# Shared down product in three rounded terms, and a new order of the second expert's weight loads

## The reference

```python
scores = softmax(x_flat @ gate_w.T); w = scores * in_top2
h = silu(g) * u                    # per expert, I = 352
out = sum over experts of (h @ experts_down[e].T) * w[:, e]
shared = (silu(x_flat @ shared_gate_w.T) * (x_flat @ shared_up_w.T)) @ shared_down_w.T   # SI = 704
out = out + sigmoid(x_flat @ shared_expert_gate_w.T) * shared
```

## Time and profile before

| | |
|---|---|
| median of 3 runs | 480.49 us (479.61 to 480.49) |
| the profiled execution | 479.78 us, of which the span in the trace is 478.1 us |
| PE busy | 462.0 us, 97% of the span |
| DVE, ACT, POOL busy | 287.1, 201.8, 242.8 us |
| chain that ended last | PE 83%, DVE 6%, ACT 4%, issue 2%, DMA 2% |

### The profile page before, as it was taken

One profiled execution on the slowest core, in us unless ns is written; L12 is line 12 of the kernel. 1 busy time (PEld: TensorE's weight loads), 2 busy tenths in 40 slices (PEclk: granted clock), 3 DMA queues, 4 the chain that ended last, 5 costly groups with the idle time before them and its releaser, 6 DMA issues.

```text
span 478.1 us, 9570 instructions
## 1 busy us (share of the span) xinstructions
PE 462.0 (97%) x3166; PEld 382.7 (80%) x3166; DVE 287.1 (60%) x651; ACT 201.8 (42%) x452; POOL 242.8 (51%) x324
## 2 busy tenths in 40 slices
PE   7999999999999999999999999999998899999996
PEld 6777767687777788779999999999987667767685
DVE  5879986562353122335455545545556779999895
ACT  3555775477620022003332332233232555676752
POOL 6323443155337557267895553233231665766654
PEclk9999999999999999999999999999999999999999
DMA  8999600020002223999913333222116400000104
GB/s 275 388 411 353 96 13 1 1 88 2 0 1 93 85 70 107 309 281 218 314 38 110 101 100 89 70 68 76 47 39 203 158 1 2 2 2 0 45 14 165
DMA packets 48144, 53.00 MB, mean 111 GB/s; under 512 B 15425, under 2 KB 42370, under 8 KB 47842
## 3 DMA queue, kind: packets, MB, share of 16 engines
q1 hardware_dynamic: 38562, 29.51, 22.0%
q0 software_dynamic: 7664, 20.19, 12.7%
q10 hardware_dynamic: 1872, 2.69, 1.8%
HBM read 35.25 MB, written 17.12 MB: 110 GB/s over the span
## 4 chain that ended last, share of the span: by engine, by line
PE 83%; DVE 6%; ACT 4%; issue 2%; DMA 2%; POOL 0%; SPq 0%; ACTq 0%; POOLq 0%; DVEq 0%
PE banks L1263 12%; PE banks L1316 10%; PE banks L347 6%; PE banks L1367 6%; PE banks L325 5%; PE banks L1368 5%; PE banks L1371 5%; PE banks L361 5%; PE banks L314 4%; PE banks L336 3%; PE banks L1389 3%; PE banks L1390 3%; PE banks L1393 3%; PE banks L1379 3%; PE banks L978 2%
## 5 line engine op out<-in xcount | busy, mean ns | idle before, releaser
L1201 ACT ACTIVATE hg<-banks 128x352 f32<-128x352 f32 x39 | 18.1, 465 | 98.4 <-PE banks L1371 98.4
L115 POOL TENSOR_TENSOR rstd<-var,mhalf 128x2 f32<-128x2 f32 x30 | 20.8, 695 | 74.7 <-DVE var L108 74.7
L1541 DVE TENSOR_TENSOR hgT_lo<-banks,hgT_hi 128x256 fp32r<-128x256 f32 x78 | 24.1, 350 | 56.3 <-ACT hgT_hi L1208 56.3
L1367 PE MATMUL banks<-w_hi,xgT_hi 128*128 x156 | 54.7, 351 | 0.1
L515 DVE TENSOR_REDUCE mx<-banks 128x16 f32<-128x1024 f32 x32 | 39.1, 1221 | 20.9 <-PE banks L325 20.7
L1368 PE MATMUL banks<-wd,xgT_hi 128*128 x156 | 50.3, 323 | 0.0
L1316 PE MATMUL banks<-sdn,big 128*128 128x256 f32 x192 | 47.5, 393 | 0.0
L1316 PEld LDWEIGHTS banks<-sdn,big 128*128 128x128 f32 x192 | 34.1, 189 | 12.6 <-issue 9.0
L1098 POOL DMA_INDIRECT expert_rows_in<-xn,slot x32 | 31.4, 980 | 18.4 <-issue 6.7
L325 PE MATMUL banks<-kvb,qT 64*128 64x256 f32 x256 | 36.3, 401 | 2.2 <-DVE pw L518 0.9
L1371 PE MATMUL banks<-w_hi,xgT_lo 128*128 x156 | 37.6, 322 | 0.0
(11 more groups left out here) (250 smaller groups left out, 1163.8 us busy)
## 6 DMA issues: line engine op xcount, KB each, us to landing
w_hi<-in_egu POOLq DMA_DIRECT2D x2, 2816.0 KB, 21.6
expert_rows_in<-zeros SPq DMA_DIRECT2D x1, 5304.0 KB, 40.9
xn<-expert_rows_in SPq DMA_DIRECT2D x39, 128.0 KB, 2.1
y_all<-choices_out SPq DMA_DIRECT2D x16, 256.0 KB, 5.2
wd<-in_egu SPq DMA_DIRECT2D x4, 704.0 KB, 7.2
out_x<-x SPq DMA_DIRECT2D x7, 256.0 KB, 2.3
x<-in_x SPq DMA_DIRECT2D x2, 768.0 KB, 7.4
wd<-in_edown POOLq DMA_DIRECT2D x4, 384.0 KB, 6.6
```

Source lines behind the costliest of these rows:

```text
L1367: nc.tensor.matmul(to, xgT_hi[:, c, k, :], hi, start=(k == 0), stop=False)
```

## The change

It does four things. (1) The shared down product is done in three terms, as the others are: ACT rounds the hidden rows (`high_part`) and the weights `sdn` (`round_shared_down`), POOL (slices 0 to 7) or DVE (the rest) makes the hidden rows' low part (`low_part`), DVE that of the weights (`split_shared_down`), and `down(g)` has 72 products of float32r. `hidden` is now on DVE for all slices, and ACT's copy of the up half is gone. (2) `down(0)` stands ahead of `up(8)`, where it stood behind `up(11)`, and `rank_choices` stands behind `up(8)`. (3) Expert 1's weights are loaded by SP and POOL after `down(2)` is done (`d_ready` 12) instead of by ACT and POOL after `up(23)`; their low parts are both made by POOL, `make_w_lo(1)` no longer by DVE. (4) The weights of the second attention are loaded behind all experts' weights, since their memory holds `sdn_hi` now, and the list `products` is weighted anew.

```diff
+        weights_at = nc.sbuf_base - 3 * KD * D * 4
+        hT_hi, hT_lo, hT_more, sdn_hi, sdn_lo = [
+            nc.alloc_sbuf_tensor_at(name, shape, F32R, offset=at) for name, shape, at in (
+                ("hT_hi", [P, KS, SG], big_at), ("hT_lo", [P, KS, SG], big_at + KS * SG * 4), ("hT_more", [P, 2, 2, SG], turned_at),
+                ("sdn_hi", [P, KS, D], weights_at), ("sdn_lo", [P, KS, D], sdn_at))]
...
+        act_s = mem["pw"]
+        FACTORS, BY_POOL = 4, 8
+        HELD_IN = [0, 1, 2, 3, 4, 5, 6, 7, 0, 1, 2, 3, 4, 5, 8, 9, 6, 7, 0, 1, 2, 3, 10, 11]
+        def h_part(n, lo):
+            at = HELD_IN[n]
+            if at < KS:
+                return (hT_lo if lo else hT_hi)[:, at, :]
+            if at < KS + 4:
+                return (xn2T_lo if lo else xn2T_hi)[(at - KS) // 2][:, (at - KS) % 2, :]
+            return hT_more[:, at - KS - 4, lo, :]
+        def wait_low_part(engine, n):
+            if n < BY_POOL:
+                wait(engine, h_done, n + 1)
+            else:
+                wait(engine, h2_done, n - BY_POOL + 1)
...
-            wait(sp, events["q_ready"], Q_STEPS)
-            wait(sp, events["wo_ready"], NU)
-            for dst, src in ((wk, wk1), (wv, wv1), (wq[1], wq1), (wo[1], wo1)):
-                sp.dma_start(dst[:, :, :], split(src)).then_inc(attn1_in, 16)
             sp.wait_ge(scattered, 16 * 2 * NT)
             for b in range(NX):
                 fetch(sp, b)
+            sp.wait_ge(d_ready, 12)
             sp.wait_ge(d_in, 16 * KI)
-            sp.wait_ge(w_in[1], 16 * KD)
+            load_w(sp, 1, 2, w_in[1])
+            load_d(sp, 1, 2, 1, d_in)
+            sp.wait_ge(d_in, 32 * KI)
             load_w(sp, 2, 4, w_in[2])
             load_d(sp, 2, 4, 1, d_in)
             for b in range(NX, NX + 3):
                 fetch(sp, b)
-            sp.wait_ge(h2_done, 2 * KS)
-            sp.wait_ge(ranked, 1)
+            sp.wait_ge(d_ready, 16)
...
+            for dst, src in ((wk, wk1), (wv, wv1), (wq[1], wq1), (wo[1], wo1)):
+                sp.dma_start(dst[:, :, :], split(src)).then_inc(attn1_in, 16)
             for b in range(NX + 5, NB):
                 fetch(sp, b)
...
+            def low_part(n):
                 rows = slice(0, SR[n % KS])
-                wait(pool, silu_done, n + 1)
-                wait(pool, u_copied, n + 1)
-                nc.gpsimd.tensor_tensor(hT[rows, (n // KS + 1) % 2, n % KS, :], up_s[rows, n % 2, :],
-                                        act_s[rows, n % 2, :], ALU.mult).then_inc(h_done, 1)
+                wait(pool, hi_done, n + 1)
+                nc.gpsimd.tensor_tensor(h_part(n, 1)[rows, :], act_s[rows, n % FACTORS, :], h_part(n, 0)[rows, :].bitcast(F32),
+                                        ALU.subtract).then_inc(h_done, 1)
...
-            downs = lambda first, end: [(d_ready, n, 11) for n in range(first, end)]
-            products = downs(1, 5) + halves(2 * KS, 2 * KS + 2) + downs(5, 9) + halves(2 * KS + 2, 4 * KS - 2)
+            downs = lambda first, end: [(d_ready, n, 10) for n in range(first, end)]
+            products = halves(2 * KS - 1, 2 * KS + 2) + downs(5, 9) + halves(2 * KS + 2, 4 * KS - 1)
...
-            pool.wait_ge(h2_done, 2 * KS)
-            load_d(pool, 0, 2, 0, d_hi_in[0])
+            pool.wait_ge(h2_done, 4 * KS - BY_POOL)
+            load_d(pool, 0, 1, 0, d_hi_in[0])
             pool.wait_ge(d_hi_in[0], 16 * KI)
-            pool.wait_ge(w_in[1], 16 * KD)
+            pool.wait_ge(d_ready, 12)
+            load_d(pool, 1, 2, 0, d_hi_in[0])
+            pool.wait_ge(d_hi_in[0], 32 * KI)
             load_d(pool, 2, 5, 0, d_hi_in[0])
             pool.wait_ge(w_hi_in, 16 * KD)
+            pool.wait_ge(lo_made, 1)
+            pool.wait_ge(w_in[1], 16 * KD)
+            make_w_lo(nc.gpsimd, 1)
             pool.wait_ge(d_lo_made, 1)
-            pool.wait_ge(d_in, 16 * KI)
+            pool.wait_ge(d_in, 32 * KI)
+            pool.wait_ge(d_hi_in[0], 32 * KI)
             make_d_lo(nc.gpsimd, 1)
-            pool.wait_ge(lo_made, 2)
...
+                if n >= FACTORS:
+                    wait_low_part(act, n - FACTORS)
+                nc.scalar.activation(act_s[factor_rows(n), n % FACTORS, :], gate_at(n)[0:SR[n % KS], :], ACT.Silu).then_inc(silu_done, 1)
+            def high_part(n):
+                rows = slice(0, SR[n % KS])
+                if n == 1:
+                    wait(act, events["wo_ready"], NU)
+                if n >= 8:
+                    wait(act, d_ready, 8 if n >= 16 else 4)
+                wait(act, t_done, n + 1)
+                nc.scalar.activation(h_part(n, 0)[rows, :], act_s[rows, n % FACTORS, :], ACT.Copy).then_inc(hi_done, 1)
+            def round_shared_down():
+                act.wait_ge(shared_in, 80)
+                wait(act, events["wo_ready"], NU)
+                for rows, ks in ((slice(0, P), slice(0, KS - 1)), (slice(0, SR[5]), slice(KS - 1, KS))):
+                    nc.scalar.activation(sdn_hi[rows, ks, :], sdn[rows, ks, :], ACT.Copy).then_inc(sdn_ready, 1)
+            for n in range(4 * KS):
...
+                if n > 0:
+                    high_part(n - 1)
...
+                if n == 6:
+                    round_shared_down()
...
             load_w(act, 0, 1, w_in[0])
-            load_d(act, 0, 2, 1, d_in)
-            load_w(act, 1, 2, w_in[1])
+            load_d(act, 0, 1, 1, d_in)
...
-                wait(nc.tensor, u_copied, n - 1)
+                wait(nc.tensor, t_done, n - 1)
...
+                pe.wait_ge(sdn_ready, 4)
+                wait_low_part(pe, KS * g + KS - 1)
+                terms = [(x, w, j) for j in range(KS) for x, w in ((0, sdn_hi), (0, sdn_lo), (1, sdn_hi))]
                 for c in range(2):
                     wait(pe, sh_added, 4 * g + 2 * c - 2)
                     for t in range(2):
-                        for j in range(KS):
+                        for m, (x, w, j) in enumerate(terms):
                             last = nc.tensor.matmul(psum[4 + c][:, t * D:(t + 1) * D],
-                                                    hT[0:SR[j], (g + 1) % 2, j, (2 * c + t) * P:(2 * c + t + 1) * P],
-                                                    sdn[0:SR[j], j, :], start=(j == 0), stop=(j == KS - 1))
+                                                    h_part(KS * g + j, x)[0:SR[j], (2 * c + t) * P:(2 * c + t + 1) * P],
+                                                    w[0:SR[j], j, :], start=(m == 0), stop=(m == len(terms) - 1))
...
-            for n in range(2, 2 * KS):
+            for n in range(2, 8):
...
+            down(0)
+            up(8)
+            rank_choices()
+            for n in range(9, 2 * KS + 2):
...
+        def hidden(n):
+            bank, rows = up_at(n)
+            wait(nc.vector, silu_done, n + 1)
+            wait(nc.vector, u_ready, ups(n + 1))
+            nc.vector.tensor_tensor(act_s[0:SR[n % KS], n % FACTORS, :], bank[rows, :], act_s[rows, n % FACTORS, :],
+                                    ALU.mult).then_inc(t_done, 1)
+        def split_shared_down():
+            nc.vector.wait_ge(sdn_ready, 2)
+            for rows, ks in ((slice(0, P), slice(0, KS - 1)), (slice(0, SR[5]), slice(KS - 1, KS))):
+                nc.vector.tensor_tensor(sdn_lo[rows, ks, :], sdn[rows, ks, :], sdn_hi[rows, ks, :].bitcast(F32),
+                                        ALU.subtract).then_inc(sdn_ready, 1)
...
+            hidden(1)
             stats2(5)
             stats2(6)
-            for u in range(3, NU):
+            split_transposed(3)
+            stats2(7)
+            for u in range(4, NU):
+                hidden(u - 2)
                 split_transposed(u)
-                if u == 3:
-                    stats2(7)
+            hidden(6)
+            split_shared_down()
+            hidden(7)
...
+            add(0)
+            hidden(8)
...
+            hidden(9)
...
+            hidden(10)
+            low_part(8)
...
+            low_part(9)
+            for n in range(11, 4 * KS):
                 hidden(n)
-            add(1)
...
+                low_part(n - 1)
+                if n == 2 * KS + 1:
+                    add(1)
+            low_part(4 * KS - 1)
...
             add(2)
-            dve.wait_ge(w_in[1], 16 * KD)
-            make_w_lo(v, 1)
```

More of the change, by code:

```diff
@@ L1193, in scalar_on @@
                     nc.scalar.activation(col["sg"][:, :], lg[:, :, E], ACT.Exp, scale=-1.0).then_inc(ex_done, 1)
-            for n in range(2 * KS, 4 * KS):
-                silu(n)
+            high_part(4 * KS - 1)
             def silu_rows(b):
@@ L1331, in tensor_on @@
                     logits(LOGITS_AT[n])
-            down(0, (0, rank_choices))
-            for n in range(2 * KS, 2 * KS + 2):
+            down(0)
+            up(8)
+            rank_choices()
+            for n in range(9, 2 * KS + 2):
                 up(n)
@@ L1459, in add, with low_part @@
```

(6 more changed lines are left out.)

53 lines of the change are left out of this document (13 added, 40 removed).

## The result

The changed kernel takes 484.11 us (median of 4 runs, 483.97 to 484.49) where the kernel before takes 480.31 beside it: a ratio of 1.0096, 95% interval 1.0082 to 1.0109. It is slower; 474.3 was predicted. The profiled execution took 483.97 us with a span of 482.3, against 478.1 before: 4.2 more.

What follows compares the result with a forecast made beforehand. The prediction took PE's own list and its waits as the bound, with 8 to 12 us of cover over the loads. The third block moving from 219.3 to 213.8 took 5.5 off 479.8, giving 474.3 us; range 470.2 to 478.8.

Steps and rivals of the forecast that it cites:

- From there on nothing is late: Behind the third block: expert 2's low parts ready at about 225, wanted by PE at 232.3; no further loss.
- The second attention's weights [...] cost nothing: Loads of the second attention's weights: made more than 100 us before their use, costing nothing.
- The down product: Each of four shared downs on PE: 72 products at 0.118 us, 8.5 us against 11.73, 3.2 less.
- The gross gain: Four shared down products on PE, each 3.2 us shorter: 12.9 us.
- Down(0): Start of down(0): PE waits 0.9 us for the split shared down weights, bounds 0 and 2.2.
- The scatter: POOL's scatter, with its eleventh transfer tied to down(1)'s end: done at 196.2, including 0.6 us for DVE's low_part.
- Rival (d): DVE's low_part holds up POOL's scatters by its whole length, 6.2 us, not 0.6; 479.9 us; chance 0.04.
- the wait for `make_w_lo(1)` at the third block: Third expert block: PE waits 4.5 us for expert 1's low part, made by POOL behind three loads.
- the first landing: First of POOL's loads for expert 1 behind the scatter: lands 3.5 us after the end of its issue.
- the second: Second of POOL's loads for expert 1, meeting SP's loads of its other weights: lands in 4.3 us.
- The third block: Third expert block, the first of expert 1: begins at 213.8 and not at 219.3.
- Rival (b): Clock halves in PE's 4.5 us wait at the third block: 1.9 to 3.7 us more, 476.2 to 478.0; chance 0.14.

Runs made afterwards that it cites:

- a0: The changed kernel as it is, run again beside its variants; 485.07 us, ratio 1.0123 to the kernel before.
- e5: Changed kernel with second attention's weights behind block 19's fetch and block 4's fetch ahead of the load of experts 2 and 3; 481.26 us, 1.0041.
- e2: Changed kernel with the four loads of the second attention's weights behind block 19's fetch instead of ahead of block 9's; ratio 1.0001.
- e14: The kernel of e2 run once more; 483.05 us, ratio 1.0036.
- e7: e5 with down(0) behind up(8) and the terms of every second token tile of a down in reverse order; 477.26 us, 0.9963.
- e13: Changed kernel with down(0) behind up(8) alone; 485.08 us, ratio 1.0068.
- e12: Changed kernel with block 4's fetch alone ahead of the load of experts 2 and 3; 488.41 us, ratio 1.0147.
- e10: e7 with block 9's fetch ahead of experts 6 and 7's load, make_w_lo(1) on DVE, make_w_lo(0) behind add(2) and the scatter; 477.11 us, 0.9882.
- e4: Kernel before with the second attention's four weight loads behind all experts' weights and ahead of block 9's fetch; ratio 1.0017.
- e3: Changed kernel with fetches of blocks 4 and 5 ahead of experts 2 and 3's load, and attention weights behind block 19's fetch; ratio 1.0103.

## Why the prediction was wrong

**The steps that failed**, with 7.1 of the 9.7 us, are "From there on nothing is late" and "The second attention's weights [...] cost nothing". I had followed POOL's list to its end and PE's, but SP's only to its first fetches. SP waits for PE before each further fetch (`bt_ready`), and behind each wait stand megabytes of loads; the loads in turn keep the next fetches back. Of the loads I had taken only their own use as their due time. What stands behind them in the queue was due first: PE came for block 4's tokens at 223.3 and for block 9's at 245.9, and on the prediction's own numbers it was to come for block 9 near 239.7 (213.8 and seven blocks of 3.7). What the runs show in place of that step: waits of 2.72 and 2.32 us for these tokens with half clock behind the first, and 7.1 us lost behind the third block. The step from a0 to e5, on one calm chip, took 3.8 us off by SP's order alone; e2 and e14 point the same way for the attention weights, across chips and beside standstills. That block 4's fetch has a part of its own is shown by e5's profile, not by a time.

**The down product**, 8.5 us, was mis-sized: 9.9. A product is 0.12, as I took it from the earlier trace rows; but each change of 128 to 64 rows and back costs two gaps of 0.1, four per token tile. e7 halved their number and won 0.6 per down. The gross gain was 4 x 1.8 = 7.2 and not 12.9, before the half clock in down(0).

**Down(0)**: the wait was 2.0, within my bounds of 0 to 2.2 (0.9 taken), but I had not asked what it does to the clock: 3.5 us at half rate, 1.7 lost. I had put the clock's rival at one wait, the third block's, and it came at two others. Together with the products PE reached the experts at 210.1 and not 203.5.

**The scatter** was done at 200.2 and not at 196.2. The eleventh transfer, which I tied to the end of down(1), went out at 166.12, 0.8 behind that end (165.28) and 0.30 behind the tenth; the waits that the profile shows are those of the sixth and seventh, for earlier parts of the same `down`. So the tie to PE was there, and what failed is when PE gets to the end of down(1): 5.9 us later than the 159.4 of the prediction, of which the wait at down(0) makes 1.1, the half clock 1.7 and two downs 2.8. This comes back in part by faster landings, 1.5 us behind the last issue in both rounds where I had 3.6 and 4.0; and the second round is 2.6 longer than its 20.2 by the issues that DVE held, where I had taken 0.6.

**Rival (d)**, the port, is right as a mechanism, and its size lies between my 0.6 and the rival's 6.2. All issues together took 1076 ns in the mean against 980, 3.1 us more over 32, and the longer ones are those that begin while DVE subtracts, with 512 columns as with 1408. The Trainium skill, "SBUF — State Buffer", section "SBUF: two separate sides", lets VectorE with two SBUF inputs hold up a GpSimd operation that reads SBUF for the whole instruction, where VectorE starts first. The traces agree: the 92 issues held took what was left of the subtraction plus 0.85 us.

**What held**: the wait for `make_w_lo(1)` at the third block (1.84; 4.5 predicted, as PE came later), the first landing of 3.4 (3.5), the second of 5.3 (4.3). The third block was to be at 213.8; the 4.2 that it came later are the scatter's 4.0 and little else. With the queue, `down(0)` and the tiles mended, e7 has it at 212.3 and 477.3 us, inside the range given; but its two waits (2.9 at the third block, 1.1 at block 9) and its rows differ from those forecast, so this is a kernel mended towards the prediction and no support for it.

**Rival (b)**, the clock, was right as a mechanism. The Trainium skill, "TensorE: Matmul & The Clock Gate", Part 1, has the array at half rate after enough idling; after PE's idle 2.0 us at `down(0)`, 2.7 at block 4 and, in e7, 2.9 the traces show 0.50; after the 1.84 at 217.99 and the wait at block 9 (2.3) they don't, and in e5 the same 2.0 at `down(0)` left it at 1.00. The length of the wait alone does not decide it in these traces: in a0 1.78 us at the third block were followed by 0.50, in e13 2.70 at block 4 and in e12 2.9 at block 9 were not.

## What to carry to other kernels

When a load is moved in a queue, ask for the due time of everything behind it, not its own; small fetches that an engine needs every few us go ahead of bulk loads, or on a queue without any. A fetch that itself waits for progress must not stand ahead of a load that this progress needs. A wait of PE of some 2 us can cost nearly twice its length, for the half clock that stood behind some of them and not behind others. And where DVE works on SBUF alone beside a scatter by POOL, look at what runs when each issue starts.

## What was not expected of the hardware

A transfer of 1 KB landed 10.05 us after its issue behind loads on its queue, and with loads under way one issue took SP up to 2.6 us (232.98; 0.43 at 200.59).

On three of four chips PE, ACT and DVE stood still near 190 us, with no wait that the profile shows. Waits of e10, PE's and DVE's:

```profile
PE banks L1354 <- issue: 2.5, 4, 1.1
```

```profile
DVE pw L1479 <- remote: 4.5, 1, 4.5
```

e4, made from the kernel before, has it too (DVE 7.8 us). In the kernels with float32r downs it fell into down(2), and up to 16 us at 0.50 followed (e3, 197 to 213). The Trainium skill, "Runtime: NRT & Kernel Launch", section "Instruction fetch mechanics", says that each sequencer fetches its instructions by a DMA queue of its own, mostly hidden; no run here shows whether that is what was late. The cause stays open, and so does how much of the sets' differences of 1 to 3 us it makes.
